# Out-degrees of a graph counted with 13 wide products per row of cells instead of 49 narrow ones

## The reference, cut to what matters

```python
deg_row = jnp.maximum(jax.ops.segment_sum(ones, row, num_segments=n), 1.0)   # row = src
deg_col = jnp.maximum(jax.ops.segment_sum(ones, col, num_segments=n), 1.0)   # col = dst
w = jax.lax.rsqrt(deg_row[row] * deg_col[col])
...
for _ in range(K):                                # K = 10
    out = spmm(out) * BETA + h * ALPHA
```

## Time and profile before

| | |
|---|---|
| median of 3 runs | 8985.64 us (8981.37 to 9012.94) |
| profiled execution, its own time | 9017.37 us |
| its span, first to last instruction | 9015.5 us |
| relation layers with counting | 4096 to 5453 us and 5577 to 6834 us |
| propagation | 7006 us to the end |
| PE busy over the span | 59% |
| POOL busy over the span | 37% |

### The profile page before, as it was taken

One profiled execution on the slowest core, in us unless ns is written; L12 is line 12 of the kernel. 1 busy time (PEld: TensorE's weight loads), 2 busy tenths in 40 slices (PEclk: granted clock), 3 DMA queues, 4 the chain that ended last, 5 costly groups with the idle time before them and its releaser, 6 DMA issues.

```text
span 9015.5 us, 140479 instructions
## 1 busy us (share of the span) xinstructions
PE 5276.5 (59%) x47086; PEld 4379.6 (49%) x47087; DVE 2679.7 (30%) x5950; ACT 1586.1 (18%) x3420; POOL 3320.8 (37%) x3295
## 2 busy tenths in 40 slices
PE   4535444256655557874333335333332999999998
PEld 3323222133333336863332234323322999999998
DVE  4100000277777663232222223222223211111111
ACT  1112111003455541011111111111110000000000
POOL 2354454555555430005566653665664000000000
PEclk7555555577777777986565567566665999999999
DMA  6111111622333333433222224222222666666665
GB/s 238 38 42 42 37 45 46 57 62 73 80 82 83 83 55 130 148 111 93 64 58 59 66 57 116 59 66 57 59 59 35 200 199 199 198 198 199 199 198 166
DMA packets 531454, 914.61 MB, mean 101 GB/s; under 512 B 223435, under 2 KB 365788, under 8 KB 530220
## 3 DMA queue, kind: packets, MB, share of 16 engines
q1 hardware_dynamic: 285688, 621.27, 22.4%
q0 software_dynamic: 104896, 162.89, 8.8%
q10 hardware_dynamic: 140646, 128.06, 4.6%
HBM read 705.38 MB, written 205.67 MB: 101 GB/s over the span
## 4 chain that ended last, share of the span: by engine, by line
PE 50%; issue 18%; another core or an unknown queue 17%; DVE 7%; DVEq 3%; ACT 3%; DMA 1%; POOL 0%; ACTq 0%; SPq 0%; POOLq 0%
PE bank L1343 26%; PE bank L1226 7%; PE bank L1297 4%; DVEq L513 2%; PE bank L1070 2%; PE bank L1368 1%; PE bank L1322 1%; PE bank L1215 1%; PE bank L1361 1%; DVE edge_sums L1766 1%; PE bank L1132 1%; ACT staged_records L830 1%; PE bank L1120 1%; PE bank L1135 1%
## 5 line engine op out<-in xcount | busy, mean ns | idle before, releaser
L731 POOL DMA_INDIRECT rows<-relation_table,staged_rows x1664 | 1681.5, 1011 | 1941.3 <-DMA staged_rows<-table_rows_of_tiles 1451.6
L1343 PE MATMUL bank<-own_term,h_transposed 128*128 128x192 f16 x16464 | 1377.7, 247 | 105.4 <-DMA h_transposed<-edge_counts 60.6
L1343 PEld LDWEIGHTS bank<-own_term,h_transposed 128*128 128x128 fp8e4 x16464 | 1364.3, 98 | 106.8 <-issue 106.0
L731 POOL DMA_INDIRECT rows<-node_table,records_in x832 | 882.2, 1060 | 766.0 <-PE bank L1215 515.4
L716 POOL DMA_INDIRECT rec_dst<-staged_records,staged_record_rows x781 | 750.9, 961 | 906.0 <-ACT staged_record_rows L839 522.5
L1343 PE MATMUL bank<-own_term,staged_records 128*128 128x192 f16 x12348 | 1032.4, 246 | 0.0
L1343 PEld LDWEIGHTS bank<-own_term,staged_records 128*128 128x128 fp8e4 x12348 | 1020.0, 98 | 0.0
L1766 DVE TENSOR_TENSOR edge_sums<-edge_sums,bank 128x96 f32 x1664 | 421.4, 253 | 1990.8 <-PE bank L1297 1604.4
L1368 PE MATMUL bank<-ones,staged_records 128*128 128x1 bf16 x2401 | 137.9, 165 | 1203.8 <-issue 990.2
L1297 PE MATMUL bank<-rows,onehot 128*128 128x96 f32 x3328 | 592.0, 348 | 301.9 <-issue 150.0
L992 ACT CAST staged_records<-bank 128x512 fp8e4<-128x512 f32 (+1 forms) x637 | 336.8, 565 | 2284.6 <-PE bank L1361 1234.2
(11 more groups left out here) (310 smaller groups left out, 6150.8 us busy)
## 6 DMA issues: line engine op xcount, KB each, us to landing
h_transposed<-edge_counts SPq DMA_DIRECT2D x280, 784.0 KB, 4.2
staged_records<-edge_counts SPq DMA_DIRECT2D x210, 784.0 KB, 4.2
h_transposed<-edge_counts_T SPq DMA_DIRECT2D x56, 784.0 KB, 4.3
rec_dst<-records_in SPq DMA_DIRECT2D x80, 520.0 KB, 10.8
records_in<-rec_dst SPq DMA_DIRECT2D x104, 400.0 KB
edge_counts_T<-staged_records ACTq DMA_DIRECT2D x343, 112.0 KB
staged_records<-edge_counts_T ACTq DMA_DIRECT2D x49, 784.0 KB
edge_counts<-staged_records ACTq DMA_DIRECT2D x49, 784.0 KB
```

The costliest lines, as they stand in the source:

```text
L731: pool.indirect_dma_start(out=rows[:, g, j, 0:D], out_offset=None, in_=source, in_offset=at(ap=index(g, j), axis=0)).then_inc(gathered[g], 16)
L1343: last = nc.tensor.matmul(banks[j][:, 0:2 * D], slots[c][:, at:at + P], z[:, c * SB + i, :], start=(c == 0 and i == 0), stop=(c == SG - 1 ...
```

## The change

Before, each of the 49 blocks of `turn_out` is the stationary operand of a product with a column of ones, and the result is a column of 128 counts, one node a partition: `banks[7][:, b]`. After, `turn_out` is the moving operand, 512 columns at a time, and the stationary operand is 128 by 13 with ones in one column and zeros elsewhere: `count_in_row` shifted by the group's number q. So group q's column sums are added to row q of bank 7, and zeros to the other twelve rows. 49 pairs of weight load and product become 13.

The counts now lie as 13 rows of 512. Once, after the last round, DVE copies them to `degree_rows` (in the memory of `onehot`), before the last normalisation; PE turns them with four transposes into bank 4; DVE copies them to `deg["src"]` with two copies instead of one. The memset of bank 7 covers 13 rows of 512 in place of 128 by 49, and the operand of ones is set up by three memsets in place of one. The semaphore `turn_read` is now `rows_counted`, `feat_ready` is `operand_made`; both have one more step at the end.

```diff
-                        for b in range(NB):
-                            last = nc.tensor.matmul(banks[7][:, b:b + 1], turn_out[:, b * P:(b + 1) * P], ones_8[:, :],
-                                                    start=False, stop=True, skip_group_check=True)
-                        last.then_inc(turn_read, 1)
+                        for q in range(TURNS):
+                            w = min(4, NB - 4 * q) * P
+                            last = nc.tensor.matmul(banks[7][0:TURNS, 0:w], count_in_row[:, TURNS - 1 - q:2 * TURNS - 1 - q],
+                                                    turn_out[:, 4 * q * P:4 * q * P + w], start=False, stop=True,
+                                                    skip_group_check=True)
+                        last.then_inc(rows_counted, 1)
...
+                pe.wait_ge(operand_made, 4)
+                pe.wait_ge(turn_kept, NB * TURNS + 1)
+                for j in range(4):
+                    last = nc.tensor.transpose(banks[4][:, j * TURNS:(j + 1) * TURNS], degree_rows[:, j * P:(j + 1) * P],
+                                               ident[0:TURNS, 0:TURNS])
+                last.then_inc(rows_counted, 1)
...
-            V.memset(ones_8[:, :], 1.0)
+            V.memset(count_in_row[:, 0:TURNS - 1], 0.0)
+            V.memset(count_in_row[:, TURNS:2 * TURNS - 1], 0.0)
+            V.memset(count_in_row[:, TURNS - 1:TURNS], 1.0)
...
-                then(V.memset(banks[7][:, 0:NB], 0.0))
+                then(V.memset(banks[7][0:TURNS, :], 0.0))
                 norm(3, h)
                 for l in range(2):
                     relation_layer(l, (1 + l) * ROUNDS)
+                dve.wait_ge(rows_counted, NB + 1)
+                V.tensor_copy(degree_rows, banks[7][0:TURNS, :]).then_inc(operand_made, 1)
                 norm(4, h)
-                dve.wait_ge(turn_read, NB + 1)
-                then(V.tensor_copy(deg["src"][:, :], banks[7][:, 0:NB]))
+                dve.wait_ge(rows_counted, NB + 2)
+                then(V.tensor_copy(deg["src"][:, 0:NB - 1].rearrange("p (q j) -> p j q", j=4),
+                                   banks[4][:, 0:4 * TURNS].rearrange("p (j q) -> p j q", j=4)[:, :, 0:TURNS - 1]))
+                then(V.tensor_copy(deg["src"][:, NB - 1:NB], banks[4][:, TURNS - 1:TURNS]))
```

More of the change, by code:

```diff
@@ L198, in build @@
         onehot = sb("onehot", [P, 2, GT * P])
+        degree_rows = onehot[0:TURNS, 0, 0:BANK]
         idx_st = sb("staged_rows", [P, SLOTS, GT], I32)
@@ L294, in build @@
         w2s = sb("L1_W2_scaled", [D, D])
-        ones_8 = sb("ones_16", [P, 1], BF16)
+        count_in_row = sb("ones_in_one_column", [P, 2 * TURNS - 1], BF16)
         we_diag = sb("We_diag", [P, 4 * D])
@@ L430, in build @@
         sum_added = sem("sum_added")
-        feat_ready = sem("feat_ready")
+        operand_made = sem("operand_made")
         feat_ps = sem("feat_ps")
@@ L435, in build @@
         turn_kept = sem("turn_kept")
-        turn_read = sem("turn_read")
+        rows_counted = sem("rows_counted")
         turn_out_done = sem("turn_out_done")
@@ L985, in keep_turned @@
                     act.wait_ge(turn_out_done, row * 16 + 16)
-                    act.wait_ge(turn_read, row + 1)
+                    act.wait_ge(rows_counted, row + 1)
                     act.sem_inc(begun, 1)
@@ L1366, in turn @@
                         pe.sem_inc(begun, 1)
-                        for b in range(NB):
-                            last = nc.tensor.matmul(banks[7][:, b:b + 1], turn_out[:, b * P:(b + 1) * P], ones_8[:, :],
-                                                    start=False, stop=True, skip_group_check=True)
-                        last.then_inc(turn_read, 1)
+                        for q in range(TURNS):
[4 more added lines that the diff above has]
+                        last.then_inc(rows_counted, 1)
                 pe.sem_inc(slot_free, SG - 1)
                 pe.sem_inc(bank_done, SB)
-                pe.sem_inc(turn_read, 1)
+                pe.sem_inc(rows_counted, 1)
                 pe.sem_inc(turn_kept, 1)
@@ L1380, in _ @@
                     if k:
-                        pe.wait_ge(feat_ready, 3)
+                        pe.wait_ge(operand_made, 3)
                     project(k, w2s if k else w1b, 1 + k)
@@ L1384, in _ @@
                     if not k:
-                        pe.wait_ge(feat_ready, 1)
+                        pe.wait_ge(operand_made, 1)
                         nc.tensor.transpose(tbank[0][0:D, 0:P], feat_max[:, 0, :], ident[:, :])
                         nc.tensor.transpose(tbank[0][0:D, P:2 * P], feat_max[:, 1, :], ident[:, :]).then_inc(feat_ps, 1)
-                        pe.wait_ge(feat_ready, 2)
+                        pe.wait_ge(operand_made, 2)
                         nc.tensor.matmul(banks[7][:, 0:D], feat_b[:, :], ident[0:D, 0:D], start=True,
@@ L1924, in _ @@
                 then(V.tensor_scalar(feat_max[:, 1, :], feat_max[:, 1, :], -1.0, None, ALU.mult))
-                dve.sem_inc(feat_ready, 1)
+                dve.sem_inc(operand_made, 1)
                 dve.wait_ge(feat_ps, 1)
```

## The result

On the chip of the first measurement the changed kernel takes 8839.7 us (median of 4 runs, 8816.3 to 8855.9) against 8988.5 us for the kernel before (median of 4 runs there, 8981.4 to 9012.9): ratio 0.9824, 95% interval 0.9803 to 0.9845. The prediction said 9016 us (8860 to 9110) with 0.27 for faster. The rival "the gain stays" is what happened, and with more gain than it was priced at. What follows calls "late" a round with a pause of POOL over 12 us behind it, and "ordinary" any other.

A forecast was written before the change was run, and what follows sets the result against it. The relation layers were taken as bound by a chain of waits, with POOL pausing 11.2 us a round. Alternating pauses (25 us), first rounds (4) and DVE work (1) added 30 us to 8985.6, giving 9016 us, range 8860 to 9110.

The forecast's parts named there:

- the gain stays: Rival: short pauses don't make the next round late, so 42 rounds gain 3.1 us each, 8861 us; chance 0.27.
- The slow path and the pause: POOL's 11.2 us pauses await slot 0's sum; PE's instructions or completions pass 0.7 us apart until gathers stop, unprofiled too.
- The counting products, in an ordinary round: 72 fewer PE instructions let count and sum run within the gathers; pause 3.1 us shorter (2.4 to 3.7), 8.1 us.
- What it sets off: A short POOL pause makes the next round late; there the new count costs net 2.2 us, giving a 15.5 us pause.
- likeliest case: Short and long POOL pauses alternate, averaging 11.8 us against 11.2: 25 us more over 42 rounds; chance 0.46.
- A late round's price: Count behind the gathers costs 4.0 us more, sum less at a risen clock: net 2.2 us (1.4 to 4.0).
- The rest: Layers' first rounds cost 4 us (0 to 8), DVE's copies and memset 1 us (0.5 to 2); other parts hidden.
- Nothing moves: Rival: slot 0's sum stays where it is, only five late rounds pay 2.2 us, 9002 us; chance 0.15.

The follow-up runs named there:

- group 2: Changed kernel and versions without counting products beside the kernel before, on a chip where it takes 7883 us; the changed kernel's ratio is 1.0001.
- group 5: Kernel before (9073 us), changed kernel without counting products or wait ahead of slot 0's sum (0.9851), and changed kernel gathering 96 bytes a row (0.9882), on one chip.
- 12 and 36 extra pairs: Changed kernel with 12 or 36 more pairs of weight load and one-column product behind each row's count: ratios 0.9918 and 1.0044 to the kernel before.
- quarter rows: Changed kernel with relation-layer gathers of 96 bytes a row instead of 384: ratio 0.9882 to the kernel before.
- narrow: Kernel before with only 13 of its 49 one-column counting products: ratios 0.9861 and 0.9870 to the kernel before, on two chips.
- none: Changed kernel without any counting product, PE's wait for the last copied piece kept: ratio 0.9867 to the kernel before on a chip with slow completions.
- the count moved: Changed kernel with each row's count moved behind the next round's sum of slot 0: ratio 0.9872 to the kernel before.
- group 4: Changed kernel (0.9873), kernel before with 13 narrow products (0.9870) and changed kernel without counting products (0.9867), on one chip where the kernel before takes 9063 us.
- group 5's kernel without products: Changed kernel without counting products, PE's wait for the last copied piece moved behind slot 0's sum: ratio 0.9851 to the kernel before.

## Why the prediction was wrong, by its own steps

**The slow path and the pause.** Right, and now shown. In the changed kernel sum to load is 0.14 us in every round on a chip without it, and up to 20.4 us with it. It is in the timed runs too and no effect of the profile: whole runs take 7885 us where the profile has pauses of 0.3 us, and 8985 to 9090 us where it has 11 to 12. The pauses are not all of that difference. Between the kernel before in the first measurement and in group 2 there are 1128 us of span, of which 602 lie ahead of the relation layers and 531 in them.

**The counting products, in an ordinary round.** The mechanism was right. In 38 of the 40 ordinary rounds count and sum ran within the slow stretch, and the load left when it ended. The size was off: the forecast took 3.1 us, between 2.4 and 3.7, and a pause of 8.1 us. Measured is 10.96 to 7.24 us, 3.7, and periods 3.77 and 3.63 us shorter. The upper bound, 3.7 us less through an end 2.6 us after the opening, was the value to take (2.75 above). The lower one came from rounds that were half early, with pauses of 8.44 and 8.84 us. Of the 40 ordinary rounds of the changed kernel only two (pauses of 8.51 and 7.79 us) still have SP's load directly behind the sum.

**What it sets off: the step that failed.** The likeliest case let short and long pauses take turns and so charged 21 late rounds. It read "a short pause makes the next round late" from three rounds of three. The rounds of the changed kernel follow a pause under 9 us forty times, and two of the forty are late. On the chip of group 5 neither of two such rounds of the kernel before is late, and 15 of its 40 others are. Over six traces other than the one predicted from (changed twice, 12 and 36 extra pairs, before, quarter rows) 28 of 122 rounds behind a short pause are late and 39 of 130 behind a longer one. With the three other traces in which PE waits ahead of the sum (narrow twice, none) it is 47 of 212 and 50 of 166. So the pause isn't the cause. What decides is when the last copy of the row before ends, 43 us or more into the round or ahead of that; and with PE's wait for it moved off the sum no late round is left (one, of 12.04 us, with the count moved). What sets when that copy comes stays open. The number of PE instructions doesn't order the late rounds (17 with 50 counting instructions, 9 to 12 with 26 or fewer on the later chips, 12 with 98, and 5 and 15 with the 98 of the kernel before), and the same changed kernel has 2 late rounds on one chip and 9 on another. The rival's reason, fewer instructions to get through, is not shown by this.

**A late round's price.** The count was priced at 5.4 us against 1.45, the sum behind it at less through the risen clock, net 2.2 us. Both late rounds of the changed kernel, in the timeline of PE, and then its granted clock in windows, the first three of the first round, the last two of the second (the column before the last two):

```profile
6270.68 5.38 PE L1370 MATMUL bank<-staged_records,ones_in_one_column 128*13 128x512 fp8e4 x13 [23.21 <-ACT staged_records L993]
6276.00 2.14 PE L1298 MATMUL bank<-rows,onehot 128*128 128x96 f32 x16
...
6375.74 4.24 PE L1370 MATMUL bank<-staged_records,ones_in_one_column 128*13 128x512 fp8e4 x13 [20.45 <-ACT staged_records L993]
6379.91 2.02 PE L1298 MATMUL bank<-rows,onehot 128*128 128x96 f32 x16
```

```profile
6270.00:6273.00 3.00, 2.32 (x6) 0.78 (x7) 0.00 (x0) 0.27 (x1) 0.00 (x0) 0.50 0.40 70
6273.00:6276.00 3.00, 3.00 (x9) 0.80 (x7) 0.00 (x0) 0.00 (x0) 0.00 (x0) 0.50 1.04 339
6276.00:6278.00 2.00, 2.00 (x18) 2.00 (x18) 0.00 (x0) 0.00 (x0) 0.00 (x0) 0.93 0.55 189
...
6375.00:6378.00 3.00, 2.25 (x6) 0.80 (x7) 0.00 (x0) 0.47 (x2) 0.00 (x0) 0.50 0.41 60
6378.00:6380.00 2.00, 2.00 (x10) 0.67 (x7) 0.00 (x0) 0.00 (x0) 0.00 (x0) 0.83 1.03 303
```

In the first 5.38 - 1.45 is 3.9 us more, 3.73 - 2.14 is 1.6 us back: net 2.3 us, as priced. In the second the clock rises within the count, which takes 4.24 us, and 1.1 us are left. The second kind is the commoner: the counts of the nine late rounds of group 4's changed kernel take 4.1 to 5.4 us, 4.7 on average. What a late round pays is read best from the end of the copy that it waited for to POOL's next gather. That is 8.3 us on average in the kernel before (both traces) and in the narrow one (both), 9.5 us in the changed kernel's two late rounds and 9.4 us in group 4's nine. So the term is 1.1 to 1.3 us on average, under the 1.4 to 4.0 us of the forecast. The pauses are shorter still than this says, 13.55 and 13.04 us where 15.5 were forecast, because the copies ended 45.0 and 45.8 us into the round instead of 46.5 to 47.2. The price was charged to 21 rounds where two paid.

**The rest.** The layers' first rounds lost nothing, where 4 us were charged: the third round of the first layer fell from 58.4 to 53.7 us, that of the second stayed (54.0 and 53.9). From the last round of the layers to the end the changed kernel lost 1.2 us, 1 us forecast. The sum of the difference: a layer's start 3.7 us earlier (not laid to the change: in the later groups on chips with the slow path it lies anywhere from 4110 to 4136 us), 4.7 us in that third round, 156 us in the 42 rounds, 3.7 us in the round behind them, less 5.6 us in the last round of the first layer and the way to the second, less 1.2 us at the end, makes the 161. The 5.6 us are mostly that last round, whose sums end 67.4 us into it instead of 63.5; the kernel before does so too in group 5 (66.3), so I don't lay it to the change.

**The rivals.** "The gain stays" with 3.7 us in place of 3.1 and without the 5 us would have said 8985.6 - 155 = 8830 us; measured 8839.7. "Nothing moves" is what two other chips showed, by a reason that no rival had: they lack the slow path, so the pause to be won is 0.3 us. One trace couldn't tell that.

The Trainium skill (Advanced Engine Details and Errata, Engine Queue Depths) gives TensorE a queue of 64 instructions. From 4942.80 on 38 pairs, 76 instructions, ran in one go, against 66 in the earlier trace rows. In the 8.2 us that they took, one instruction every 0.7 us is 12 more, and 64 and 12 are 76: the trace agrees if the queue is filled at the slow pace meanwhile, which no run here isolates.

## What to carry to other kernels

When a pause ends with a completion that is late by tens of microseconds, take away instructions that stand ahead of it, count what is gained up to the moment at which completions come through again, and expect nothing beyond: here 98 to 26 instructions gave all, 26 to 0 nothing. A pattern read from three cases of three in one trace deserves a rival of equal weight, above all if the event that it is tied to (here the last copy) can be read directly. And a gain that lives in a wait should be measured on more than one chip: this one is 1.8, 1.3 and 0.0% by chip.

## What the hardware showed beyond that

The kernel before takes 7883 to 7888 us in two groups and 8989 to 9090 us in the first measurement and the three other groups, 14 to 15% apart, with equal gathers (1008 and 1011 ns each). In the layers a round takes 42 us there and 53 here. Here, while POOL issues them, SP's load left up to 20.4 us behind the sum that it waits for (up to 24.9 us in group 5's kernel without products, 25.4 us with the count moved), and the trace records the semaphore's updates as late. PE's instructions run 0.7 us or a multiple of it apart once some have gone through at once; there the load followed the sum by 0.14 us. From the first gather of the last round to the end, which is mostly the propagation without gathers, both take about the same, 2131 and 2128 us. Fetching 96 instead of 384 bytes a row changed nothing that the runs can tell. I didn't find out what differs between the chips, whether it is the chip or how the program and its buffers lay on it, nor whether fewer gathered rows would open the path; that wasn't tried.
